# GpSimd, in place of VectorE, makes the high and low parts of x in a pipelined kernel of a convolution and a block-quantised feed-forward

## The reference

```python
def fp4_linear(x, w):
    return jnp.einsum('bsk,nk->bsn', fp4_quant_dequant(x), fp4_quant_dequant(w))
...
xn = _layernorm(x, axis=-1)
s = convolution(xn) + xn * D
h = silu(fp4_linear(xn, w_gate)) * fp4_linear(xn, w_up)      # 704 columns
g = silu(fp4_linear(h, w_down))                              # 256 columns
return x + s * g
```

## Time and profile before

| | |
|---|---|
| time, median of 3 runs | 587.93 us (586.7 to 588.83) |
| the profiled execution | 586.48 us, of which 584.7 us are the profile's span |
| TensorE busy | 473.7 us, 81% |
| VectorE busy | 544.3 us, 93% |
| ScalarE busy | 407.2 us, 70% |
| GpSimd busy | 198.4 us, 34%, 302 instructions |
| granted TensorE clock, mean | 0.971 of full speed |
| step 4 to step 8 begins (L799) | 153.60 to 211.03 us |
| step 8 to step 28 begins | 211.03 to 503.61 us |

### The profile page before, as it was taken

How to read it: one execution, slowest core, us unless ns; L and a number is a source line. 1 busy time by engine, 2 the same in 40 slices (tenths; PEclk the granted TensorE clock), 3 DMA queues, 4 the chain that set the end, 5 groups by cost and what they waited for, 6 DMA issues and landing times.

```text
span 584.7 us, 13233 instructions
## 1 busy us (share of the span) xinstructions
PE 473.7 (81%) x4956; PEld 331.3 (57%) x4956; DVE 544.3 (93%) x689; ACT 407.2 (70%) x568; POOL 198.4 (34%) x302
## 2 busy tenths in 40 slices
PE   0000356668999999999999999999999999998965
PEld 0000234225555567777777777777777777765654
DVE  6999999989999999999999999999999999998884
ACT  6972866889988876767676767676767666664552
POOL 1094000474555551111111111333333333137870
PEclk9999957989999999999999999999999999999998
DMA  5990012225222335353534353535354535339978
GB/s 173 349 281 1 1 36 90 91 27 163 91 91 91 109 83 159 102 146 108 149 105 142 112 147 103 144 111 146 104 143 114 144 107 148 110 59 154 172 104 132
DMA packets 101186, 70.80 MB, mean 121 GB/s; under 512 B 8848, under 2 KB 100752, under 8 KB 101008
## 3 DMA queue, kind: packets, MB, share of 16 engines
q1 hardware_dynamic: 93072, 61.94, 35.8%
q0 software_dynamic: 8064, 8.13, 9.5%
HBM read 61.28 MB, written 16.91 MB: 134 GB/s over the span
## 4 chain that ended last, share of the span: by engine, by line
PE 57%; DVE 24%; issue 9%; POOL 6%; ACT 3%; DMA 0%; SPq 0%; DVEq 0%; POOLq 0%; ACTq 0%
PE ps L1224 27%; PE ps L1242 10%; PE ps L1244 5%; PE ps L1233 5%; PE ps L1257 4%; PE ps L1261 4%; DVE wgu L944 4%; DVE work L857 2%; DVE sm L799 2%; POOL gbuf L516 2%; DVE work L883 2%; PE ps L1212 2%; DVE work L852 2%; DVE xh L919 1%; DVE xh L912 1%
## 5 line engine op out<-in xcount | busy, mean ns | idle before, releaser
L1224 PE MATMUL ps<-wgu,work 128*128 128x512 f16 (+1 forms) x1152 | 242.7, 366 | 17.1 <-DVE work L883 15.9
L1224 PEld LDWEIGHTS ps<-wgu,work 128*128 128x128 f16 x1152 | 109.9, 99 | 128.0 <-issue 17.5
L615 ACT ACTIVATE work<-ps,con 128x704 f32<-128x704 f32 x64 | 54.2, 847 | 95.1 <-PE ps L1224 95.0
L1242 PE MATMUL ps<-wdh,work 128*128 128x256 f16 x704 | 87.9, 274 | 5.5 <-ACT gbuf L619 4.7
L610 ACT COPY work<-ps 128x1408 f16<-128x1408 f16 x64 | 84.7, 1325 | 2.1 <-PE ps L1233 1.9
L852 DVE SCALAR_TENSOR_TENSOR work<-work 128x960 f32<-128x960 bf16 (+2 forms) x67 | 71.8, 1110 | 1.6 <-ACT work L630 1.5
L1242 PEld LDWEIGHTS ps<-wdh,work 128*128 128x128 f16 x704 | 65.4, 98 | 13.4 <-issue 5.3
L516 POOL TENSOR_TENSOR gbuf<-gbuf,xh 128x256 f32<-128x256 f32 (+1 forms) x42 | 41.0, 1048 | 92.0 <-DVE work L865 77.8
L857 DVE SCALAR_TENSOR_TENSOR work<-work 128x1920 f16<-128x1920 bf16 (+3 forms) x36 | 69.7, 1936 | 1.2
L818 DVE TENSOR_TENSOR work<-work,ps 128x960 f32<-128x960 f32 (+2 forms) x63 | 68.4, 1126 | 1.1
L630 ACT ACTIVATE work<-work 128x960 bf16<-128x960 f32 (+2 forms) x67 | 61.8, 960 | 9.3 <-DVE work L818 8.7
(11 more groups left out here) (153 smaller groups left out, 675.1 us busy)
## 6 DMA issues: line engine op xcount, KB each, us to landing
work<-kpad SPq DMA_DIRECT2D x64, 512.0 KB, 3.8
work<-L_attn_u SPq DMA_DIRECT2D x33, 256.0 KB, 3.0
gbuf<-u_rev SPq DMA_DIRECT2D x4, 2048.0 KB, 18.6
out<-gbuf POOLq DMA_DIRECT2D x7, 1024.0 KB, 9.5
out<-L_attn_u SPq DMA_DIRECT2D x1, 768.0 KB, 5.5
out<-gbuf POOLq DMA_DIRECT2D x1, 768.0 KB, 8.1
work<-L_ffn_w_down SPq DMA_DIRECT2D x1, 704.0 KB, 6.6
work<-L_ffn_w_gate SPq DMA_DIRECT2D x1, 640.0 KB, 4.7
```

What stands on the lines that cost most here:

```text
L1224: last = T.matmul(p_gu[:, a:b], xT[par][:, t, c, :], wgu[:, part, c % 2, a:b], start=(n == 0), stop=(n == len(todo) - 1))
L1242: T.matmul(dst, hT[t][:, c, :], wdh[:, c, :], start=(c == 0), stop=False)
```

## The change

GpSimd gets a function `x_parts` that issues the same two multiplications, and calls it in steps 0 to 27 behind its tables, ahead of `a_low` and `gated`. It waits for the tables' own semaphore, for `x_r` (the rounding, VectorE's L857) and for TensorE's transposes of the pair that had the buffer before. VectorE leaves its `x_parts` out in these steps; its loop is cut in two, steps 4 to 27 without and 28 and 29 with `x_parts`. What waits for `x_hl` is unchanged.

```diff
+        X_POOL = NP - 4
...
+            def x_parts(p, par):
+
+                pool.wait_ge(x_r, p + 1)
+                after(pool, x_tp, p - 1)
+                for part, scale in enumerate((shi, slo)):
+                    q, o, sc = part_of(XH, xhl[par], part, H, scale)
+                    nc.gpsimd.tensor_tensor(o, q, sc, ALU.mult).then_inc(x_hl, 1)
...
             for it in range(NP):
                 tables(it, it < NP - 2, it >= 1)
+                if it < X_POOL:
+                    pool.wait_ge(tb_p, it + 1)
+                    x_parts(it + 2, it % 2)
                 if it < NP - 2:
                     pool.wait_ge(x_hl, 2 * (it + 3))
...
-            def step(it, par, x, gu, ch, first=True):
+            def step(it, par, x, gu, ch, first=True, x_pool=False):
...
-                if x:
+                if x and not x_pool:
                     own.settle()
                     x_parts(it + 2, par)
...
-                step(it, it % 2, True, True, it >= 1, it >= 1)
+                step(it, it % 2, True, True, it >= 1, it >= 1, x_pool=True)
...
-            loop(PEEL, NP - 2)
+            loop(PEEL, X_POOL, True)
+            loop(X_POOL, NP - 2, False)
```

More of the change, by code:

```diff
@@ L1112, in _, with loop @@
                 start = own.n
-                step(it, it % 2, True, True, it >= 1, it >= 1)
+                step(it, it % 2, True, True, it >= 1, it >= 1, x_pool=True)
             per_step = own.n - start
-            def loop(s0, s1):
+            def loop(s0, s1, x_pool):
                 start = own.n
@@ L1120, in loop @@
                         own.n = q * (2 * per_step) + (start + par * per_step)
-                        step(q * 2 + (s0 + par), par, True, True, True)
+                        step(q * 2 + (s0 + par), par, True, True, True, x_pool=x_pool)
                 own.n = start + per_step * (s1 - s0)
-            loop(PEEL, NP - 2)
+            loop(PEEL, X_POOL, True)
+            loop(X_POOL, NP - 2, False)
             step(NP - 2, 0, False, True, True)
```

## The result

The changed kernel takes 608.74 us (median of 4 runs, 607.49 to 609.22) against 587.32 for the kernel before (586.4 to 588.83): a ratio of 1.0364, 95% interval 1.0343 to 1.0385. It is slower by 21.4 us. The profiled execution took 608.82 us, its span is 607.0 us, against 584.7 before.

A forecast was written before the change was run, and what follows sets the result against it. VectorE paces steps 4 to 7, TensorE steps 8 to 27 with VectorE close behind. Loop +25.8, first steps +2, tail -2: +26 us on 586.48 gives 612.3, against the median 613 us; 8-in-10 range 590 to 621.

The forecast's parts named there:

- Both engines' two-input reads hold each other, in turns: After the rounding, GpSimd's parts and VectorE's L891 hold each other; +1.32 us a loop step, 24 steps +25.8 us; chance 0.60.
- The parts' length: Each of GpSimd's two 512-element multiplications for x takes 1.20 us, range 1.04 to 1.29.
- Who starts first: After the rounding in loop steps, GpSimd starts ahead of VectorE's L891 by 0.1 us.
- GpSimd's lateness costs nothing: In loop steps, GpSimd's later subtractions and tables still finish before VectorE wants the tables; cost 0.
- VectorE first, as a rival: After the rounding VectorE starts first, only its second L891 held 1.01 us; 14.68 us a step, 595 us, chance 0.18.
- The tail gives 2 us back: From step 28 on, L516 starts some 3 us earlier and VectorE's 2.13 us wait for tables goes: -2 us, or 0.
- Its last step: Converting the profiled execution's 612.3 us to the runs' median, 1.45 us higher: 613 us.
- The forecast of a gain in steps 0 to 7: Rival: L891 and the parts do not collide; 0.67 us gained in each of 8 steps, 5.4 us, 582.5 us; chance 0.09.

The follow-up runs named there:

- three fillers: Changed kernel with three tiny write-only GpSimd fills, each waited for, ahead of the parts of x; 591.74 us, ratio 1.0077 to the kernel before.
- h first: Changed kernel, but GpSimd makes the parts of x only after both of VectorE's products for h; 593.46 us, ratio 1.0101 to the kernel before.
- one filler: Changed kernel with one tiny write-only GpSimd fill between its wait for the rounding and the parts of x; 607.97 us, ratio 1.0359 to the kernel before.

## Why the prediction was right

It said 613 us against the median, with the mechanism above; 608.74 was measured, a change of +21.4 us where its sum had +25.8. By its own steps:

- **Both engines' two-input reads hold each other, in turns.** Right, and shown: reads hold, writes do not, a changed order frees exactly one L903. The release 0.13 us before the recorded end, read from the earlier trace rows, came back as 0.14. So the Trainium skill's rule in "SBUF — State Buffer", "Who interferes with whom", that VectorE with two SBUF inputs contends with a GpSimd instruction that reads SBUF and not with one that only writes it, agrees with these runs (3.34 us for the pair beside reads, 1.70 beside writes). The words "for the whole instruction", which the prediction quotes, stand in that section in the sentence on VectorE's two-port modes; taken over to the two-input instructions here they are 0.13 to 0.14 us too long by the recorded durations.
- **The parts' length.** This is the term that was mis-sized: 1.20 us was taken, 1.05 measured. It was at the low bound that L525 of the kernel before gave (1.04), not at L498's slope. That bound follows from the slope between the two forms of that line, (5.43 - 2.58) / (3072 - 1408) = 1.71 ns an element; the prediction's 1.77 is the larger form's whole time over its elements. With 1.05 us the sum's own steps give 14.34 + 1.0 a step; measured was +1.04. Steps 4 to 27 cost 62.84 + 307.69 - 350.0 = +20.5 us, not +25.8.
- **Who starts first.** Right from step 4 on, with a lead of 0.04 to 0.07 us and not 0.1. In the written-out steps 1 to 3 VectorE was first: GpSimd's pair takes 3.34 to 3.43 us there, its first part held, and 2.72 from step 4 on. Steps 0 to 3 cost 52.90 - 50.63 = +2.3 us (said: 2).
- **GpSimd's lateness costs nothing.** Nearly. In step 4, where the written-out steps had left GpSimd late, the tables still ran at L864 and stretched the pair to 2.72 us from 2.22; from step 5 on nothing.
- **VectorE first, as a rival.** It had 14.68 us a step and 595 us. The run with three fillers, where VectorE was first, gave 14.53 and 14.76 us in turn and 591.74. Its +2 us for 20 steps of 0.05 us should have been +1.
- **The tail gives 2 us back.** Wrong. GpSimd's and VectorE's timelines after:

```profile
542.29 1.44 POOL L525 TENSOR_TENSOR gbuf<-gbuf,xh 128x256 f32<-128x256 f32 x2 [10.35 <-ACT xh L653]
...
553.81 1.70 DVE L903 TENSOR_TENSOR work<-work,sm 128x1408 f16<-128x1408 f16 x2 [2.05 <-POOL sm L499]
```

L525 starts 15.88 us after step 28 begins (526.41), where L516 started 16.46 after it. It was taken for TensorE's backlog, but it is the place of the last convolution in the step's order of work; VectorE's wait in step 29, which is in the loop and which the prediction expected to go, is 2.05 us in place of 2.13. The tail gave 0.5 us.

20.5 + 2.3 - 0.5 = 22.3 us, the difference of the spans. The errors of the parts' length and of the tail have opposite signs: without the tail's wrong 2 us the forecast would have been further off, and in that part it was lucky. Its last step, 612.3 + 1.45, is 613.75 and not 613. The forecast of a gain in steps 0 to 7, if only nothing collided, needs one more condition that the prediction did not have: its 582.5 us took the tables to be in time. With h first the reads do not collide at L903, and the early steps still lose; only with GpSimd's other work cut did they gain.

## What to carry to other kernels

Before moving work to an idle engine, look at when its input is ready and what the relieved engine does at that moment: here both consumers of one result were released together and read through the same door, so 2.1 us of moved work cost its giver 1.71 us to save 0.67. If the work must move, make it wait until the critical engine is past its two-input instructions, or let that engine start first. Letting VectorE start first halved the hold here but did not bring a gain (591.74 us against 587.15). And price the relief stage by stage: where TensorE sets the pace it is worth nothing, and where VectorE sets the pace GpSimd must have the room inside the same quiet window, not only in its busy share.

## What the runs showed of the hardware

Who started first was served first, however small the recorded lead. With one filler GpSimd led by 0.00 to 0.04 us from step 4 on, and the first L905 was held in every step (1.76 to 1.80 us); with three VectorE led by 0.40 to 0.43 us, and it was not (0.89). That is 16 us of the whole. The changed kernel has both orders: from step 4 on GpSimd led by 0.04 to 0.07 us, but in steps 2 and 3 VectorE led by 0.05 and 0.04, and GpSimd was held. Step 3:

```profile
152.50 0.89 DVE L903 TENSOR_TENSOR work<-work,sm 128x1408 f16<-128x1408 f16 x1
152.54 1.76 POOL L510 TENSOR_TENSOR work<-work,sm 128x512 f16<-128x512 f16 x1 [2.25 <-issue]
```

TensorE's granted clock fell for some microseconds after TensorE had waited: 1.73 us for the held L903 in the changed kernel, 2.08 us for GpSimd's subtraction in the run with h first. The changed kernel in steps 5 and 6, and the run with h first in step 8 (the value behind the bracket of POOL is the granted clock; 1.00 is 2.4 GHz):

```profile
172.00:187.00 15.00, 12.74 (x100) 8.24 (x98) 14.68 (x13) 12.85 (x18) 9.93 (x12) 1.00 0.25 87
187.00:193.00 6.00, 5.90 (x30) 2.73 (x28) 5.82 (x7) 3.60 (x6) 5.61 (x8) 0.72 0.01 3
```

```profile
214.00:222.00 8.00, 5.82 (x56) 3.62 (x55) 7.86 (x10) 4.28 (x5) 7.76 (x7) 0.93 0.34 100
222.00:226.00 4.00, 4.00 (x43) 2.99 (x42) 2.97 (x2) 1.05 (x2) 3.77 (x4) 0.71 0.43 131
```

A mean of 0.72 lies between the two levels, 1.2 and 2.4 GHz. In the changed kernel one gate_up of 18 matmuls took 5.41 us there instead of 3.73, and the step 16.18 us instead of 15.39. The run with one filler shows the same in its step 6 (5.41 us, a step of 16.23). In the run with only the early steps on GpSimd, which has the same instructions there and the same wait of TensorE (1.72 us), the clock stayed at 1.00 and the step was 15.38. Why it fell in some executions and not in the other stays open; no run was made for it.
